# Cross-attention of a decoder layer: the query tiles of a head quad taken from t=7 down to t=0 instead of from t=0 up

## The reference

```python
q = (query @ Wq.T + bq)   # likewise k, v; then split into 16 heads of 32
QEr = einsum('bhsd,ld->bhsl', q, Er)
Srel = skew(QEr)          # row s of QEr shifted, so that column t holds distance s - t
attn = (q @ k.T + Srel) / sqrt(32)
attn = where(causal, attn, -inf); attn = softmax(attn)
out = attn @ v
```

## Time and profile before

| | us |
|---|---|
| median of 3 runs (lowest, highest) | 5207.08 (5204.09, 5207.57) |
| the profiled execution | 5213.15 |
| its span, first to last instruction | 5211.3 |
| relative stream, first batch | about 730 to 872 |
| attention stream, first batch | 879.5 to 1107.5 |

### The profile page before, as it was taken

One profiled execution on the slowest core, in us unless ns is written; L12 is line 12 of the kernel. 1 busy time (PEld: TensorE's weight loads), 2 busy tenths in 40 slices (PEclk: granted clock), 3 DMA queues, 4 the chain that ended last, 5 costly groups with the idle time before them and its releaser, 6 DMA issues. The chain is left out here.

```text
span 5211.3 us, 71736 instructions
## 1 busy us (share of the span) xinstructions
PE 4484.7 (86%) x27610; PEld 2598.6 (50%) x27610; DVE 2253.8 (43%) x4664; ACT 1830.0 (35%) x3492; POOL 896.5 (17%) x1001
## 2 busy tenths in 40 slices
PE   3999998869999988789999977799998882999993
PEld 1555644535565445455654455466554551444441
DVE  0444534644444336534443356344433566222224
ACT  1444413634444226434442256244422561000000
POOL 0222200102222001022221011122210010222221
PEclk9999998979999999899999989899998996999996
DMA  6111137541011175421010754311005651444445
GB/s 214 37 42 42 40 117 261 163 167 41 29 42 43 61 289 172 135 90 42 36 42 35 268 187 134 124 42 40 29 34 218 219 169 53 119 121 121 121 121 161
DMA packets 222826, 576.12 MB, mean 111 GB/s; under 512 B 11888, under 2 KB 61168, under 8 KB 219504
## 3 DMA queue, kind: packets, MB, share of 16 engines
q1 hardware_dynamic: 205664, 521.97, 28.7%
q0 software_dynamic: 14656, 34.61, 3.5%
q10 hardware_dynamic: 2304, 16.78, 0.8%
HBM read 379.99 MB, written 210.11 MB: 113 GB/s over the span
## 5 line engine op out<-in xcount | busy, mean ns | idle before, releaser
L356 POOL TENSOR_SCALAR sc<-sc,pinv 128x1024 f32<-128x1024 f32 x512 | 572.3, 1118 | 1891.9 <-DVE pinv L595 1879.4
L392 ACT ACTIVATE sc<-sc,nmax 128x1024 f32<-128x1024 f32 x512 | 588.0, 1149 | 331.9 <-DVE nmax L587 331.9
L796 PE MATMUL psum<-xt,w_all 128*128 128x512 f32 x1024 | 460.2, 603 | 152.1 <-PEq L793 152.1
L841 PEld LDWEIGHTS psum<-ident,sc 128*128 128x128 f32 x4096 | 444.1, 141 | 213.8 <-issue 157.3
L820 PE MATMUL psum<-xk,xq 64*128 64x512 f32 x2048 | 508.8, 615 | 44.0 <-ACTq L391 38.0
L841 PE MATMUL psum<-ident,sc 128*128 128x128 f32 x4096 | 515.2, 277 | 22.5 <-PEq L832 22.5
L693 DVE CUSTOM_DVE_ANT_0 sc<-psum,big 128x896 f32<-128x896 f32 (+7 forms) x512 | 373.1, 748 | 300.4 <-PE psum L984 273.0
L851 PE MATMUL psum<-pts,xv 128*64 128x256 f32 x4096 | 484.4, 384 | 7.5 <-ACT pts L424 7.5
L587 DVE CUSTOM_DVE_ANT_0 sc<-psum,table_a 128x1024 f32<-128x1024 f32 x256 | 313.5, 1225 | 402.6 <-PE psum L820 402.6
L424 ACT COPY pts<-psum 128x512 f32<-128x512 f32 x512 | 295.8, 578 | 514.1 <-PE psum L841 514.1
L602 DVE COPY pts<-psum 128x512 f32<-128x512 f32 x512 | 348.6, 681 | 293.6 <-PE psum L841 290.0
(11 more groups left out here) (136 smaller groups left out, 5109.5 us busy)
## 6 DMA issues: line engine op xcount, KB each, us to landing
big<-skew_d SPq DMA_DIRECT2D x48, 1024.0 KB, 5.0
w_sb<-w_dram SPq DMA_DIRECT2D x48, 1024.0 KB, 5.4
big<-skew_d SPq DMA_DIRECT2D x48, 768.0 KB, 4.3
table_a<-rows_d SPq DMA_DIRECT2D x32, 960.0 KB, 4.7
table_b<-rows_d SPq DMA_DIRECT2D x32, 960.0 KB, 6.1
big<-skew_d SPq DMA_DIRECT2D x32, 896.0 KB, 4.5
w_all<-wqkv_dram SPq DMA_DIRECT2D x32, 768.0 KB, 4.3
skew_d<-pts SPq DMA_DIRECT2D x12, 2048.0 KB, 6.7
```

The costliest lines, as they stand in the source:

```text
L356: pool.tensor_scalar(sc[k % 4][:, :], sc[k % 4][:, :], pinv[:, k % 4:k % 4 + 1], 1.0, ALU.mult, ALU.mult).then_inc(probs_scaled, 1)
L392: act.activation(tile, tile, ACT.Exp, bias=least, scale=-1.0, accum_out=total).then_inc(probs_ready, 1)
L796: mm = pe.matmul(psum[:, 2 * a + n, :], w_sb[:, a, c, :], xt[:, c, HALF * n:HALF * n + HALF], start=(c == 0), stop=(c == DC - 1))
L841: mm = pe.transpose(TURN[(2 * j + half) % 3][:, P * c:P * c + P], sc[j % 4][:, col:col + P], ident[:, :])
```

## The change

Within each quad the tiles are taken as t = 7, 6, ..., 0 in both streams. `ORDER` is that list; `CHUNKS` and `UNITS` are built from it, and the tile's number becomes v = 8 qd + `ORDER.index(t)`. So v, the buffers, `skew_d[v]`, and the two positions in SP's queue (behind tile 12 and tile 15) keep their numbers but stand for other tiles: tile 12 is t=3 where it was t=4, tile 15 is t=0 where it was t=7. Quads and units keep their number and size; what each computes is the same.

```diff
-CHUNKS = [(t, n) for t in range(ST) for n in range(0, P * (t + 1), HALF)]
+ORDER = list(reversed(range(ST)))
+CHUNKS = [(t, n) for t in ORDER for n in range(0, P * (t + 1), HALF)]
-UNITS = [(qd, t, hs) for qd in range(QUADS) for t in range(ST)
+UNITS = [(qd, t, hs) for qd in range(QUADS) for t in ORDER
          for hs in ([(0, 1, 2, 3)] if t < ST // 2 else [(0, 1), (2, 3)])]
-LAST = [max(i for i, u in enumerate(UNITS) if u[:2] == (v // ST, v % ST)) for v in range(XV)]
+LAST = [max(i for i, u in enumerate(UNITS) if u[:2] == (v // ST, ORDER[v % ST])) for v in range(XV)]
...
                 def load_skewed(u):
 
                     qd, t, heads = UNITS[u]
-                    v, w, nh = qd * ST + t, width(t), len(heads)
+                    v, w, nh = qd * ST + ORDER.index(t), width(t), len(heads)
...
                 for v in range(XV):
-                    w = width(v % ST)
-                    made = NCH * (v // ST) + max(j for j in range(NCH) if CHUNKS[j][0] == v % ST) + 1
+                    w = width(ORDER[v % ST])
+                    made = NCH * (v // ST) + max(j for j in range(NCH) if CHUNKS[j][0] == ORDER[v % ST]) + 1
...
                 def add_output(v):
 
                     pool.wait_ge(ot_scaled, v + 1)
-                    cols = xr[:, v % ST, P * (v // ST):P * (v // ST) + P]
+                    cols = xr[:, ORDER[v % ST], P * (v // ST):P * (v // ST) + P]
...
                 def xweigh(v):
 
-                    qd, t = v // ST, v % ST
+                    qd, t = v // ST, ORDER[v % ST]
```

More of the change, by code:

```diff
@@ L481, in copy_rel @@
                     t, n = CHUNKS[j]
-                    v, m = qd * ST + t, min(HALF, width(t) - n)
+                    v, m = qd * ST + ORDER.index(t), min(HALF, width(t) - n)
                     act.wait_ge(rel_for_act, NCH * qd + j + 1)
@@ L499, in copy_xturned @@
                     _, t, heads = UNITS[u]
-                    m, v = TURN0[u] + g, UNITS[u][0] * ST + t
+                    m, v = TURN0[u] + g, UNITS[u][0] * ST + ORDER.index(t)
                     n = P * min(4, len(heads) * (t + 1) - 4 * g)
```

## The result

The changed kernel takes 5189.15 us (median of 8 runs, 5187.01 to 5194.23) against 5206.92 us of the kernel before (8 runs): a ratio of 0.9971, interval 0.9961 to 0.9982. It is faster by 17.8 us. The prediction was 5169.5 us, 37.6 faster. The time lies in the widest range given, 5146 to 5198, but above the forecast's own, 5155 to 5185, and the gain is less than half of what was forecast.

What follows compares the result with a forecast made beforehand. No engine was full; a unit's period was a loop through three engines. Terms -7.5 - 4.9 + 2.2 + 0.8 = -9.4 us a batch, -37.6 in four, gave 5169.5 us; own range 5155 to 5185, widest 5146 to 5198.

Steps and rivals of the forecast that it cites:

- Part 1: Relative stream, third quad: a smaller store ahead of the skewed loads nearly removes a copy's wait; -7.5 us a batch.
- The first rival: Third quad: the wait moves to tiles 19 to 23 instead of going; 5185 to 5201 us, chance 0.15.
- Part 2: Last quad to first `add_relative`: smaller last tiles shorten the change of streams; -4.9 us a batch, bounds -3.5 and -5.9.
- Part 3: Start of attention: large t=7 units now stand under the low clock; +2.2 us a batch, bounds 0 and +5.
- Part 4: Attention stream: changed unit neighbours and half-clock stretches together cost +0.8 us a batch, bounds -3 and +6.
- pairing: Attention stream: each unit's scores stand beside other units' turns and weighings; the quad's sum changes by -0.7 to +0.5 us.
- low stretches: Attention stream: half-clock periods after units in which TensorE idles, counted at 1.5 us apiece.
- the second rival: Attention stream: more TensorE idling puts half clock on large units; gain gone at 25 more stretches, 5217 us, chance 0.10.
- the signs set down: Against the forecast: waits before tiles 19 to 23, periods above 5.5 at t=2, t=1 or first t=7, attention clock under 0.9.

Runs made afterwards that it cites:

- the kernel with late loads: The kernel before, with the first four units' skewed loads issued behind tile 21 (t=5) instead of tile 15: 5201.93 us, ratio 0.9990.
- the last kernel of the experiments: The kernel before with only the relative stream downwards, identity transposes beside t=7, 6, 5, 3, 2 and 24 behind the first score burst: 5109.20 us.

## Why the prediction was right and wrong

*Part 1, the wait in the third quad.* Forecast -7.5 us a batch, measured -8.2, with +0.4 in the second quad and -0.6 in the first. The mechanism is shown by the kernel with late loads. Tile 16 was forecast to land 19 to 21.5 us after tile 15's copy; it took 19.3 (815.2, less 795.9 for the end of that copy). In that sum two errors cancel: tile 15's store took 5.1 us where 2.9 were counted, and the loads then passed in 9.2 us where 11.6 to 13.5 were. The first rival did not happen at tile 19, by 0.6 us. Tiles 21 to 23 did wait for stores, up to 2.2 us each, where the forecast had the other stores no worse and no copy idle for over 2 us; the quad lost little by it.

*Part 2, the last quad and the change of streams.* Forecast -4.9, measured -4.9. The idle time there was forecast as 3 to 4 us, ended by TensorE; it is 4.2 to 4.7, ended by the last store in three batches of four. That the sum came out exactly is in part luck. In the first batch, counted from the last quad's first matmul (831.04), the last copy ended at 30.2 us and the score burst ran from 30.4 to 34.2, as forecast; but the last store landed at 34.7, not 33.3. The time before was mis-sized as well: 879.49 - 840.0 is 39.5, not 39.2, and the quad's first matmul stood at 839.29, which gives 40.2. These errors nearly cancel.

*Part 3, the low clock at the start.* Forecast +2.2. From the first `add_relative` to the second quad it takes 53.0 us on average, 53.3 before: no loss. The large units at half clock stand there as forecast (7.60 us for the second t=7), but t=3, t=1 and t=0, moved behind them, run at full clock, and t=2 in two batches of four.

*Part 4, pairing and low stretches: this is the step that failed.* "+0.8 a batch, bounds -3 and +6" measured +7.7 (7.4 for the stream, 0.2 more without part 3), outside its own bounds. Two terms were mis-sized. The pairing was put at -0.7 to +0.5 us a quad and is +0.7. The low stretches were counted as those of before, and the text itself named the reason against it, 2.4 us of idle time beside t=3 and the first t=7: they went from 1 or 2 a quad to 3, and the new one at the second t=7 costs 2.0 to 2.6 us where 1.5 a stretch was counted. "In one piece" isn't what made it worse there: the first t=7 had a piece of 1.53 us before, with a low stretch behind it in two of twelve quads, and has 1.42 and 0.56 now, with one behind it in all. A quad loses 58.3 - 52.85 = 5.5 us to them where it lost 55.3 - 52.17 = 3.2: +2.3 us a quad. This was the second rival's mechanism, at part of its size (13 more stretches in the later quads, where it wanted 25 in all): not enough to turn the sign, enough to take half of the gain. Three of the signs set down came out against the forecast: t=2 above 5.5 us, a mean clock of 0.89, and attention above 233 us.

The sum: -37.6 forecast, -17.8 measured by medians, 19.8 apart. Parts 3 and 4 together came out 4 x (7.4 - 3.0) = 17.6 us worse than forecast, parts 1 and 2 together 4 x (13.3 - 12.4) = 3.6 better, so the stages read in the two profiles give -23.6; the two profiled executions themselves are 25.3 apart (5213.15 and 5187.84). The rest is what they differ from their medians, 6.2 above and 1.3 below. The attention stream shows such differences: the kernel before had 226.5 us of attention in its profile, and 224.9 and 225.3 in two kernels with the same units in the same order.

What stays open: why filling that holds the clock upwards does not hold it downwards beside t=7 (the unfilled 1.42 us are a candidate that no run tests), and how much of the first quad's 54 to 62 us hangs on when the clock changes relative to the work.

## What to carry to other kernels

Where an order is changed in two streams at once, price each stream by itself and try them apart: here one half brought 50 us and the other lost 33 to 36. When work is moved so that a full engine gets small work beside another's large work, look at the idle time it creates, in one piece or in several close together, and at what follows it, not only at the sum of the periods. If TensorE's idle time can't be removed, cheap matmuls put into it can be worth as much as the reordering (47 us beside 50 here), if they stand in every long piece and don't lengthen the unit.

## What the runs showed of the hardware

The granted clock fell to 0.5, again and again at the same units, in an engine that was 84% busy over the stream. In the later quads before and after the change, each fall but one came within 4 us of the start of an idle piece of 1.1 to 2.1 us (the one: pieces of 0.6 us), though not each such piece has a fall behind it. Transposes of a constant put into these gaps kept the clock at 0.99 in the last kernel of the experiments. In the Trainium skill, TensorE: Matmul & The Clock Gate, section HAM oscillation, longer idle gaps are named as what brings the low clock back; here shorter ones did, and the measurement decides.

In the full queue, skewed loads with long rows moved faster than with short ones. Before, the last of the four loads landed at 812.5, 8.4 us behind tile 15's store: 3.4 us per MB for 2.5 MB in rows of 0.5 to 2 KB. After, tile 15's store had landed at 801.15 and the last load at 810.35: 2.5 us per MB for 3.75 MB in rows of 3.5 and 4 KB. That the row length is the reason isn't shown: in the attention stream of the kernel before, a 1 MB load landed after a median of 5.1 us with rows of 2 KB (t=3) and 4.9 us with rows of 4 KB (t=7).
